# Handing out maxima, token steps and projections by time, and taking the layer-norm statistics of the later token tiles early

## The reference

```python
xn = layernorm(x)                                   # x: [2048 tokens, 256], no affine part
q, k, v = split(xn @ Wqkv.T)                        # 16 heads of 16
q, k = rope(q), rope(k)
scores = where(causal, q @ k.T * 16**-0.5, -inf)    # full causal attention over 2048 tokens
attn = softmax(scores) @ v @ Wout.T
w, idx = gate(xn)                                   # 32 experts, 4 of 8 groups, top 6, weights sum to 2.5
y = sum over the 6 experts of w * (silu(xn@w11.T) * (xn@w33.T)) @ w22.T
shared = (silu(xn @ sw1.T) * (xn @ sw3.T)) @ sw2.T
out = x + attn + y + shared
```

## Time and profile before

| | us |
|---|---|
| median of 3 runs | 893.49 (893.37 to 894.62) |
| profiled execution, its own time | 888.71 |
| its span, first to last instruction | 886.7 |
| PE busy | 817.1 (92%) |
| DVE busy | 606.5 (68%) |
| POOL busy | 505.4 (57%) |
| ACT busy | 493.5 (56%) |

### The profile page before, as it was taken

The page is one execution under the profiler, slowest core; times in us unless marked ns, Lnnn a source line. Parts: engine busy times, 40 slices in busy tenths (PEclk is TensorE's granted clock), DMA queues, the critical chain, the costliest instruction groups (busy, mean ns, idle before and its releaser), DMA issues.

```text
span 886.7 us, 17207 instructions
## 1 busy us (share of the span) xinstructions
PE 817.1 (92%) x5089; PEld 442.3 (50%) x5090; DVE 606.5 (68%) x1187; ACT 493.5 (56%) x1214; POOL 505.4 (57%) x654
## 2 busy tenths in 40 slices
PE   4799987788989989999999999999999999999997
PEld 2366554233333433377888888873343333433444
DVE  2567787888887788755555555557788787888422
ACT  3456542154556557644444444457676767667762
POOL 3556660299989730066666666626878888820000
PEclk9799997699999999999999999999999999999999
DMA  9005554720000141058777877774585555520011
GB/s 235 1 32 175 172 176 150 190 74 18 1 19 1 36 108 37 1 135 258 220 220 245 235 233 231 141 145 76 72 170 90 72 89 72 89 32 1 13 37 48
DMA packets 82624, 96.43 MB, mean 109 GB/s; under 512 B 13660, under 2 KB 74076, under 8 KB 82524
## 3 DMA queue, kind: packets, MB, share of 16 engines
q0 software_dynamic: 19968, 31.47, 19.8%
q1 hardware_dynamic: 45672, 47.10, 18.2%
q10 hardware_dynamic: 16896, 16.78, 5.6%
HBM read 61.11 MB, written 33.82 MB: 107 GB/s over the span
## 4 chain that ended last, share of the span: by engine, by line
PE 77%; DVE 12%; issue 4%; DMA 2%; DVEq 2%; ACT 1%; POOLq 1%; POOL 1%; SPq 0%; ACTq 0%
PE bank L1208 14%; PE bank L1191 13%; PE vector_banks L1283 12%; PE vector_banks L1169 12%; DVE mpart L967 9%; PE bank L1300 6%; PE vector_banks L1061 5%; PE vector_banks L1082 4%; PE bank L1082 3%; PE bank L1061 2%; DMA xn_all<-wexp 2%; PE vector_banks L1228 2%; PE bank L1098 1%; PE vector_banks L1172 1%; PE bank L1194 1%
## 5 line engine op out<-in xcount | busy, mean ns | idle before, releaser
L967 DVE TENSOR_REDUCE mpart<-vector_banks 128x2 f32<-128x1024 f32 (+3 forms) x320 | 329.7, 1062 | 79.1 <-PE vector_banks L1169 48.8
L725 ACT ACTIVATE probs<-bank 128x512 f32<-128x512 f32 (+3 forms) x428 | 212.7, 539 | 123.9 <-PE bank L1191 62.9
L1191 PE MATMUL bank<-turned 108*128 108x512 bf16 (+3 forms) x640 | 201.4, 353 | 7.6 <-DVE turned L989 2.2
L1169 PE MATMUL vector_banks<-turned 96*128 96x512 bf16 (+3 forms) x640 | 185.0, 359 | 14.6 <-DVE mpart L967 13.7
L598 POOL DMA_INDIRECT turned<-normed_rows,tok_i x128 | 125.3, 979 | 122.2 <-PE vector_banks L1061 90.4
L613 POOL DMA_INDIRECT res<-expert_rows,slot_i x96 | 148.8, 1550 | 41.7 <-issue 28.4
L725 ACT ACTIVATE at_first<-bank 128x512 f32<-128x512 f32 (+3 forms) x212 | 105.6, 533 | 67.5 <-PE bank L1194 36.4
L1191 PEld LDWEIGHTS bank<-turned 108*128 108x128 bf16 x640 | 58.2, 97 | 164.0 <-ACT probs L725 71.8
L1283 PE MATMUL vector_banks<-xn_all,probs 128*128 x512 | 135.0, 386 | 3.9 <-issue 1.6
L1208 PE MATMUL bank<-probs,V 128*32 128x512 f32 (+3 forms) x856 | 102.3, 549 | 0.0
L1283 PEld LDWEIGHTS vector_banks<-xn_all,probs 128*128 128x128 f32 x512 | 87.2, 190 | 16.5 <-issue 8.6
(11 more groups left out here) (157 smaller groups left out, 963.0 us busy)
## 6 DMA issues: line engine op xcount, KB each, us to landing
expert_rows<-probs ACTq DMA_DIRECT2D x32, 512.0 KB, 4.2
term_rows<-at_first SPq DMA_DIRECT2D x96, 128.0 KB
turned<-term_rows SPq DMA_DIRECT2D x32, 384.0 KB, 4.9
xn_all<-wexp SPq DMA_DIRECT2D x32, 384.0 KB, 4.0
normed_rows<-xn_all SPq DMA_DIRECT2D x4, 512.0 KB, 5.9
turned<-normed_rows,tok_i POOLq DMA_INDIRECT x128, 3.8
out<-res SPq DMA_DIRECT2D x16, 128.0 KB, 1.7
res<-x SPq DMA_DIRECT2D x1, 1536.0 KB, 10.8
```

The lines of the kernel that those rows point to most:

```text
L725: A(PT[v // 2 % 6][:, v % 2, 0:width], bank[A_BANK[step][0]][:, 0:width], ACT.Exp).then_inc(s["scalar_bank_read"], 1)
L967: V.tensor_reduce(mpart[:, t % TPC, 2 * j:2 * j + 2, p], ring[:, :, 0:w], AX.X, ALU.max).then_inc(s["vector_bank_read"], 1)
L1169: last = mm(ring[:, h, 0:w], q_turned(slice(0, KQ), 2 * j + h, t * P, P), k_turned(par, slice(0, KQ), 2 * j + h, p * CH, w), start=True, s ...
L1191: last = mm(ring[:, 0:CH - off], k_turned(parity(g), slice(0, KM), h, kb * P, P), q_turned(slice(0, KM), h, c * CH + off, CH - off), start ...
```

## The change

In the order: a call of `some` after an `st` now advances the clock by 6/8 of a tick, and a new call behind the place of `pv` (made in every key block, whether or not a `pv` stands there) advances it by 8/8. A key block keeps its four ticks, the goals keep their places, and there are five calls in place of four, so the routing chain gets up to ten items in a key block in place of eight. `mt` and `ot` still wait four ticks.

In the start: the rows of x come in three transfers, tiles 0 to 3, 4 to 7 (`MIDDLE`) and 8 to 15 (`LAST`), the last two right behind the weights and ahead of the rope tables, with no wait of SP; DVE takes the statistics of all later tiles right behind those of the first four, before it waits for the rope tables; ACT takes the `LATE` root in its iteration t = 0 (ahead of `proj_read(0)`) and normalizes tiles 4 and 5 in t = 1, tile 6 in t = 2.

```diff
+MIDDLE, LAST = slice(QT4, 2 * QT4), slice(2 * QT4, NT)
@@ due
-            upto = n0 + -(-(n1 - n0) * (min(at, a1) - a0) // (a1 - a0))
+            upto = n0 + int(-(-(n1 - n0) * (min(at, a1) - a0) // (a1 - a0)))
@@ whole_order
-    def some(everything=False):
+    def some(eighths, everything=False):
         nonlocal at
-        at += 1
+        at += eighths / 8
...
         order.append(("st", g, c, kb, 0))
-        some()
+        some(6)
         order.append(("st", g, c, kb, 1))
-        some()
+        some(6)
         if len(pending) == 2:
             values(pending.pop(0))
+        some(8)
         order.append(("st", g, c, kb, 2))
-        some()
+        some(6)
         order.append(("st", g, c, kb, 3))
-        some()
+        some(6)
         pending.append((g, c, kb))
-    some(True)
+    some(0, True)
@@ sync
-            load_x(EARLY)
+            load_x(EARLY, "x_in")
...
+            load_x(MIDDLE, "middle_in")
+            load_x(LAST, "last_in")
             sp.dma_start(cos_sb[:, :, :], ...)
             sp.dma_start(sin_sb[:, :, :], ...)
-            sp.wait_ge(s["x_in"], 16)
-            load_x(LATE)
@@ scalar
+                if t == 0:
+                    act.wait_ge(s["var_ready"], 2)
+                    A(root[:, LATE], var[:, LATE], ACT.Sqrt).then_inc(s["root_ready"], 1)
                 proj_read(t, t % 2, t < 2)
                 if t:
                     hidden_turned(t - 1, (t - 1) % 2, t - 1 < 2)
                 if t == 1:
-                    act.wait_ge(s["var_ready"], 2)
-                    A(root[:, LATE], var[:, LATE], ACT.Sqrt).then_inc(s["root_ready"], 1)
-                if t == 2:
                     act.wait_ge(s["scales_ready"], 2)
-                for n in ((QT4, QT4 + 1, QT4 + 2) if t == 2 else (t + QT4,) if 2 < t < NT - QT4 else ()):
+                for n in ((QT4, QT4 + 1) if t == 1 else (t + QT4,) if 1 < t < NT - QT4 else ()):
                     norm(n)
@@ vector
-            def statistics(tiles, part):
-                dve.wait_ge(s["x_in"], 16 * part)
-                for t in range(tiles.start, tiles.stop):
-                    V.bn_stats(stat[:, t, :], res[:, t, :])
+            def statistics(tiles, part, pieces):
+                for piece, arrived in pieces:
+                    dve.wait_ge(s[arrived], 16)
+                    for t in range(piece.start, piece.stop):
+                        V.bn_stats(stat[:, t, :], res[:, t, :])
...
-            statistics(EARLY, 1)
+            statistics(EARLY, 1, ((EARLY, "x_in"),))
+            statistics(LATE, 2, ((MIDDLE, "middle_in"), (LAST, "last_in")))
...
-                if t == 1:
-                    statistics(LATE, 2)
```

More of the change, by code:

```diff
@@ L383, in layer @@
         OVER_Y = (0, 1)
-        names = """x_in w_in tables_in w2_in xn_stored ident_made counts_made
+        names = """x_in middle_in last_in w_in tables_in w2_in xn_stored ident_made counts_made
             var_ready root_ready scales_ready xn_ready qk_ready xT_psum xT_ready proj_done rope_done proj_read act_ready hm_ready hT_psum hT_ready
@@ L403, in _, with load_x @@
         def _(sp):
-            def load_x(tiles):
+            def load_x(tiles, arrived):
                 sp.dma_start(res[:, tiles, :], x[tiles.start * P:tiles.stop * P, :].rearrange("(t p) d -> p t d", p=P)
-                             ).then_inc(s["x_in"], 16)
-            load_x(EARLY)
+                             ).then_inc(s[arrived], 16)
+            load_x(EARLY, "x_in")
             for dst, src, width in ((C_QK, wqkvT, 3 * D), (C_G, sw1T, D), (C_U, sw3T, D), (C_L, gateT, E)):
```

## The result

The changed kernel is slower: 900.64 us, the median of six runs (898.37 to 904.21), against 894.95 us for the kernel before in the same runs (893.37 to 896.79). The ratio is 1.0064, 95% interval 1.0045 to 1.0084. Ten further runs of each, on another chip, gave 1.0084 (1.0059 to 1.0109) for the changed kernel and 1.0024 (0.9991 to 1.0057) for the kernel before against itself. The forecast was 887.4 us, faster. The profiled execution took 901.05 us, its span 898.8.

A forecast was written before the change was run, and what follows sets the result against it. PE was taken to bound the kernel nearly everywhere (busy 92%). Terms -6.2 (start), -0.9 and +1.0 (`mt` places) gave -6.1 us: 882.6 us against the profiled execution, 887.4 against the median; range 881 to 892.5.

The forecast's parts named there:

- The start: Up to the token loop's iteration t = 3: earlier statistics and normalization were to save 3.17 + 3.0 = 6.2 us.
- The hole: PE idle from 35.6 to 38.8 us in the token loop, before `turn_row(4)`; its removal was to save 3.17 us.
- the clock's return: Token loop iteration t = 3: with PE kept busy, the lower clock would not come, saving 3.0 us.
- The covers: Before rope(0) at 19.5 us: DVE's idle 10.28 us would hide the twelve tiles' statistics, done by 18.3 us.
- The rival of late rows: Start: later rows of x land at 18.8 us, rope(0) and all behind slip 5.3 us, 892 us; 7%.
- Full key blocks: Attention key blocks with PE busy throughout were to stay at 2.85 us, cost 0.
- The rival in which the exponentials' banks make each key block wait: About 90 key blocks wait for the bank of `st` 2; at 0.12 us each, 898 us and slower; 10%.
- The opening of the attention: First four key blocks, up to 179.4 us: new interleaving taken as 0, between -5 and +3 us.
- a sign of a wrong prediction: In the changed kernel's profile, more than 35 us for the first four key blocks, or less than 32.
- The `mt` of group 0: At 205.19 us, ahead of chunk (0, 2): less cover for `mt`, costing 1.0 us, between 0 and +1.6.
- The nine later `mt` places: `mt` of (1, 3) to (3, 3): the strip after it comes one slot later, 0.1 us each, -0.9 us.
- the sixth: Attention loses some 5 us through other stops of `mt` and the routing chain, 892 us; 6%.

The follow-up runs named there:

- start_only: The kernel before with only the start of the change and the old order of steps: 889.10 us, ratio 0.9944 to the kernel before.
- start_again: The kernel before with only the start of the change, run once more on another chip: 888.80 us, ratio 0.9958.
- gathers_late: The kernel before with the new start and old order, POOL's first gather waiting for the exponential of key block (1, 2, 2): 888.78 us, ratio 0.9949.
- opening_filled: The changed kernel with idle matmuls on PE ahead of `ranks` (16), `owner` (12) and the first `st` in bank 7 (24): 898.41 us, ratio 1.0064.
- mt_sooner: The changed kernel with `mt` of chunks (0, 1), (0, 2) and (0, 3) after 3.25 ticks, not 4: 896.51 us, ratio 1.0039.
- group0_new: The kernel before with the new start, and the new order in group 0 only: 896.33 us, ratio 1.0038.
- end_new: The kernel before with the new start, and the new order in the last chunk (3, 3) only: 889.74 us, ratio 0.9959.
- group0_old: The kernel before with the new start, the old order in group 0 and the new one in groups 1 to 3: 893.87 us, ratio 1.0007.
- order_only: The kernel before with only the new order and the old start: 902.36 us, ratio 1.0095.
- start_mt: The kernel before with the new start and old order, `mt` of chunks (0, 1), (0, 2), (0, 3) after 3 ticks, not 4: 890.09 us, ratio 0.9958.
- before_again: The kernel before, unchanged, run again for a second profile: 896.34 us, ratio 1.0024.

## Why the prediction was wrong

**The start: right in kind, a term too large.** It was to win 3.17 + 3.0 us. The hole is gone and the clock is 1.00 behind it, as forecast. Measured were 4 to 5 us by time (`start_only`, `start_again`, `gathers_late`), and the first `st` comes at 138.8 to 140.7 us in the fifteen profiles with the new start, at 142.3, 142.7 and 144.8 in the three with the old. The 3.0 us of the clock's return was the term mis-sized: I took the lower clock after the hole from one execution, and the second profile of the kernel before has the same hole without it. Its timeline of PE:

```profile
37.19 0.41 PE L1061 MATMUL vector_banks<-ident,xn_all 128*128 128x128 f32 x2 [3.17 <-issue]
37.43 1.88 PE L1082 MATMUL vector_banks<-probs,turned 128*128 128x512 f32 x4
```

The four matmuls behind the hole take 1.88 us, not 3.62, and the next `turn_row` starts 6.51 us after this one, at 43.70: a steady iteration. So the 3.0 us are paid in some executions only, one of the three profiles with the old start. The covers held: statistics over at 18.82 us, rope(0) not later. (The rival of late rows adds up to 24.4 us, not 24.9: 18.8 + 2.7 + 1.0 + 1.9. It did not come.)

**Full key blocks: right.** 2.85 us in every kernel. The rival in which the exponentials' banks make each key block wait is refuted.

**The opening of the attention: the step that failed.** "I take 0, as the sum of DVE's work is what bounds it" with bounds of -5 and +3. For the first four key blocks, with more than 35 us named as a sign of a wrong prediction, the profile shows 38.3, +3.7. DVE's work is 20.2 us in three key blocks for 20.5, so it is not the bound. What bounds them is a chain of exchanges between DVE and PE in which PE's links run at either level of the clock: `ranks` at 3.41 us for 1.80. The exchanges are the same four, as forecast, but not what stands between them: one strip fewer lies between `counts` and `ranks`. Which of the two, clock or cover, costs how much is open, as said under `opening_filled`. The chain also ends two `st` sooner, not a key block. I had the earlier trace rows with its 0.75 before me and took the clock as a chance to win only. The Trainium skill, TensorE: Matmul & The Clock Gate, in "A second HAM failure mode: psum-queue depth-cycling", warns that short rests of PE between groups of matmuls, at the exchange of PSUM banks, can throw the clock back again and again. The trace agrees, with a granted clock of 0.73 over the three key blocks before and 0.61 after. A reader of it had reason to price the clock as a loss too, and I did not.

**The `mt` of group 0: right place, too small.** +1.0 us, up to 1.6, for the `mt` ahead of (0, 2). Measured: 0.6 to 1.3 there, 0.6 at the end of (0, 2), and behind it, in five of six profiles, 1.4 to 2.9 of lower clock in (0, 3, 0) and (0, 3, 1). `mt_sooner` gives back some 4 us in the profile. I followed the lost cover at one chunk and not at the next, and priced a stop without the clock that it costs. Against it stand small gains: (0, 2, 2) 0.9 us. With the 3.5 us of the opening that makes 6 to 7.5 us; group 0 costs 7.5 by time (`group0_new`).

**The nine later `mt` places: right sign, half the size, and losses beside them.** -0.9 us was expected. The nine key blocks that hold these `mt` take 37.9 us in sum after and 38.0 before, and the one at 743.17 in the earlier trace rows, from which the term was read, has now

```profile
753.20:757.47 4.27, 3.32 (x22) 0.97 (x20) 3.88 (x8) 2.07 (x4) 3.45 (x3) 1.00 0.47 67
```

4.27 us for 4.24. The key blocks right behind them are 0.4 us shorter in sum (20.56 us for 20.99, without the one that the experts stand in). What was not foreseen is that other key blocks get longer when a strip moves by a slot: (1, 2, 2) 0.4 us, (1, 3, 1) 0.3, (1, 3, 2) 0.37 (4.58 for 4.21, with 10 DVE instructions for 9 and one exponential fewer), (3, 2, 11) 0.36, in nearly every profile with the new places there. They take the gains back: without (1, 1, 4) and the experts, the medians of the middle differ by 0.4 us between the two kinds of profile. The end is 0.8 us longer in `end_new`, `group0_old` and `order_only` (59.4 us for 58.5), and 1.8 and 2.2 in the two profiles of the changed kernel, where a stretch of lower clock is added; `start_mt` has such a stretch with the old end.

By time it is 2.4 us for the middle and 0.8 for the end. The rest of the middle's 2.4 may be the longer stop in (1, 1, 4), a mean of 1.6 us, and stays open.

**The sum.** Forecast -6.2 - 0.9 + 1.0 = -6.1. Measured: start about -4.5, group 0 +7.5, the rest about +3.2 (+5 by `group0_old`): +6.2 us, and the two measurements of the ratio give +5.7 and +7.5. The case that came was the sixth, an attention that loses through stops of `mt` and the routing chain, held at 6% and at 5 us; it lost about twice that against the start. No kernel tried is faster than the start of the change alone, 0.9944 and 0.9958.

## What to carry to other kernels

Where PE and a second engine hand work to and fro in small pieces, price an order by what stands between one exchange and the next and by the time in which PE rests there, not by the sum of the other engine's work: the same fifteen matmuls cost 1.80 or 3.41 us, by the order that they stood in. Take the difference of two executions of the unchanged kernel before you explain one profile: a term read from a single one (here the 3.0 us of clock, the missing stop of 3 us, and the 2 us of (0, 1, 0)) may not be there in the next. And when a change has two parts that share no line, run them apart first: one won 0.5%, the other lost about 1%.

## What the hardware showed that was not expected

- Idle matmuls can shorten a stretch: with 52 of them (16, 12 and 24) the opening took 27.65 us for 30.92, at a granted clock of 0.75 for 0.61. A gain in the whole kernel's time is not shown. In an opening that was not slow, 28 of them changed nothing (27.5 us for 27.4).
- POOL's first eight gathers of 128 rows, about 1 us each to issue, go with a stop of PE, DVE and ACT together (in `before_again` PE 3.10 us, the key block 7.64 us for 3.05), at the start of the eighth gather and in 16 of 17 profiles. Delayed by 20 us, they cost 1.6 and 2.2 us in two key blocks. What in a gather stops the three engines is not known.
